# A layer norm's last multiply moved from GpSimd to VectorE inside a pipelined attention stage

## The reference, cut to what matters

```python
def _layernorm(x, axis=-1, eps=1e-05):
    m = jnp.mean(x, axis=axis, keepdims=True)
    v = jnp.var(x, axis=axis, keepdims=True)
    return (x - m) / jnp.sqrt(v + eps)
...
    q = (Q @ Wq.T + bq).reshape(b, vc, h, hd)
    k = (K @ Wk.T + bk).reshape(b, vc, h, hd)
    v = (V @ Wv.T + bv).reshape(b, vc, h, hd)
    atten = jnp.einsum('bqhd,bkhd->bhqk', q, k) / np.sqrt(hd)
    atten = jax.nn.softmax(atten, axis=3)
    out = jnp.einsum('bhqd,bdhv->bqhv', atten, v).reshape(b, vc, d_model)
    return out @ Wo.T + bo
...
x = _layernorm(x + _L0_xattn_ref(x, ctx_1024, ctx_1024, ...), axis=-1)
```

## Time and profile before

| | us |
|---|---|
| median of 3 runs | 2804.24 (2803.35 to 2806.08) |
| profiled execution, its own time | 2806.08 |
| its span in the profile | 2804.0 |
| mean granted TensorE clock | 0.990 |
| attention stage, roughly | 1618 to 2308 of the span |
| store of one step to the store of the next, in the loop | 84.5 |

### The profile page before, as it was taken

How to read it: one execution, slowest core, us unless ns; L and a number is a source line. 1 busy time by engine, 2 the same in 40 slices (tenths; PEclk the granted TensorE clock), 3 DMA queues, 4 the chain that set the end, 5 groups by cost and what they waited for, 6 DMA issues and landing times.

```text
span 2804.0 us, 42177 instructions
## 1 busy us (share of the span) xinstructions
PE 2692.1 (96%) x15200; PEld 2082.5 (74%) x15200; DVE 1529.3 (55%) x2566; ACT 1029.9 (37%) x2385; POOL 638.3 (23%) x564
## 2 busy tenths in 40 slices
PE   6999999999999999999999989999999979999998
PEld 4777777777778888888888767777777756777775
DVE  6887887787785221233133477777777762111222
ACT  6244244344344222122212255555555543222221
POOL 0643543553451100010001011333222331000000
PEclk9999999999999999999999999999999989999999
DMA  3011011101113101110112120111011213211111
GB/s 134 16 46 45 8 37 45 36 9 45 45 46 137 61 0 60 60 60 14 46 60 94 37 100 9 53 60 60 22 45 60 79 46 125 86 45 45 45 45 45
DMA packets 85417, 147.81 MB, mean 53 GB/s; under 512 B 3968, under 2 KB 17920, under 8 KB 85344
## 3 DMA queue, kind: packets, MB, share of 16 engines
q1 hardware_dynamic: 85344, 146.84, 15.1%
HBM read 113.27 MB, written 33.55 MB: 52 GB/s over the span
## 4 chain that ended last, share of the span: by engine, by line
PE 84%; DVE 9%; issue 2%; ACT 2%; DMA 1%; POOL 1%; DVEq 0%; SPq 0%; POOLq 0%; ACTq 0%
PE ps L75 22%; PE ps L77 21%; PE ps L76 21%; PE ps L1640 4%; PE ps L1919 4%; PE ps L730 3%; PE ps L1652 2%; DVE mx_cv L537 2%; DVE at_pT L1504 1%; PE ps L1631 1%; DVE mx_m L545 1%; PE ps L706 1%; PE ps L718 1%; DVE at_r_hl L1511 1%; PE ps L1660 1%
## 5 line engine op out<-in xcount | busy, mean ns | idle before, releaser
L1354 ACT ACTIVATE at_pr<-ps,at_nm 128x256 f32<-128x256 f32 x512 | 236.4, 475 | 199.7 <-DVE at_nm L1498 199.7
L1056 DVE TENSOR_TENSOR gm_m_lo<-gm_m,gm_m_hi 128x512 fp32r<-128x512 f32 (+1 forms) x88 | 61.0, 693 | 416.9 <-ACT gm_m_hi L973 416.9
L75 PE MATMUL ps<-sh_u_hi,gm_gu_hi 128*128 128x512 f32 (+1 forms) x704 | 275.4, 391 | 1.6 <-DVE gm_gu_lo L213 1.6
L77 PE MATMUL ps<-sh_u_hi,gm_gu_lo 128*128 128x512 f32 (+1 forms) x704 | 275.3, 391 | 0.0
L76 PE MATMUL ps<-sh_u_lo,gm_gu_hi 128*128 128x512 f32 (+1 forms) x704 | 275.1, 391 | 0.0
L1504 DVE COPY at_pT<-ps 128x512 f32<-128x512 f32 x256 | 176.0, 687 | 129.3 <-PE ps L1640 125.0
L967 ACT ACTIVATE gm_sg<-ps 128x512 f32<-128x512 f32 (+1 forms) x88 | 52.6, 598 | 520.9 <-PE ps L77 520.9
L75 PE MATMUL ps<-sh_u_hi,qm_w_hi 128*128 128x512 f32 x512 | 201.4, 393 | 3.9 <-DVE qm_w_lo L211 3.9
L76 PE MATMUL ps<-sh_u_lo,qm_w_hi 128*128 128x512 f32 x512 | 199.9, 390 | 0.0
L77 PE MATMUL ps<-sh_u_hi,qm_w_lo 128*128 128x512 f32 x512 | 199.7, 390 | 0.0
L1640 PE MATMUL ps<-sh_ident,at_pr 128*128 128x128 f32 x1024 | 164.5, 284 | 35.0 <-DVE at_pT L1504 31.9
(11 more groups left out here) (237 smaller groups left out, 6322.9 us busy)
## 6 DMA issues: line engine op xcount, KB each, us to landing
sh_xf<-x_scratch SPq DMA_DIRECT2D x16, 1024.0 KB, 7.5
sh_xf<-in_x SPq DMA_DIRECT2D x8, 1024.0 KB, 7.3
mx_xr<-in_x SPq DMA_DIRECT2D x8, 1024.0 KB, 6.3
h_scratch<-mx_xr SPq DMA_DIRECT2D x8, 1024.0 KB, 5.2
sh_xf<-h_scratch SPq DMA_DIRECT2D x8, 1024.0 KB, 7.9
gm_xr<-in_x SPq DMA_DIRECT2D x8, 1024.0 KB, 7.3
gm_r<-h_scratch SPq DMA_DIRECT2D x8, 1024.0 KB, 5.9
x_scratch<-gm_r SPq DMA_DIRECT2D x8, 1024.0 KB, 5.1
```

The source lines that it names most:

```text
L75: nc.tensor.matmul(out, l_hi, r_hi, start=first, stop=False)
L77: return nc.tensor.matmul(out, l_lo, r_hi, start=False, stop=last)
L1354: A(pr[h][:, t, :], SC[h][:, SEQ * t:SEQ * t + SEQ], ACT.Exp, bias=nm[:, 4 * n + h, t:t + 1], accum_out=sums[:, 2 * b + t, 4 * g + h:4 * g ...
```

## The change

The four instructions that subtract the mean and multiply by 1/std go from GpSimd to VectorE. On VectorE they stand in round 5, between `take_pT(i, 5, 1)` and `invert`. The fourth `statistics` and `gather` go from round 5 to round 4, and GpSimd computes 1/std behind its first `out_low`, ahead of the context's third and fourth tile. Behind the last step the same four instructions run on VectorE as well.

```diff
     def gpsimd(pool):
-        def normed(i):
-            residual_rstd(nc, pool, s, i, mv, var, rstd, eps, mhalf)
-            pool.wait_ge(s["mv"], TT)
-            pool.wait_ge(s["rstd"], i + 1)
-            for t in range(TT):
-                nc.gpsimd.tensor_scalar(r[:, t, :], r[:, t, :], mv[:, t, 0:1], rstd[:, t:t + 1], ALU.subtract,
-                                        ALU.mult).then_inc(s["ln"], 1)
...
             out_low(i, 0)
+            if not step_0(i):
+                residual_rstd(nc, pool, s, i - 1, mv, var, rstd, eps, mhalf)
             if not final(i):
                 context_low(pool, i + 1, 2)
                 context_low(pool, i + 1, 3)
             out_low(i, 1)
-            if not step_0(i):
-                normed(i - 1)
             out_low(i, 2)
...
         out_low(NP - 1, HG - 1)
-        normed(NP - 1)
+        residual_rstd(nc, pool, s, NP - 1, mv, var, rstd, eps, mhalf)
...
     def vector(dve):
+        def normed(i):
+            dve.wait_ge(s["rstd"], i + 1)
+            for t in range(TT):
+                V.tensor_scalar(r[:, t, :], r[:, t, :], mv[:, t, 0:1], rstd[:, t:t + 1], ALU.subtract,
+                                ALU.mult).then_inc(s["ln"], 1)
...
                     elif n == 4:
-                        for t in range(1, 3):
+                        for t in range(1, 4):
                             statistics(i - 1, t, before(i, 5 + t) + 1)
+                        gather(i - 1)
                     elif n == 5:
-                        statistics(i - 1, 3, before(i, 8) + 1)
-                        gather(i - 1)
+                        normed(i - 1)
...
         gather(n)
+        normed(n)
```

## The result

The changed kernel takes 2829.32 us (median of 4 runs, 2826.48 to 2830.53), the kernel before 2804.75 in the same comparison. The ratio is 1.0087, with a 95% interval of 1.0075 to 1.0100: slower by 24.6 us (21 to 28). The forecast was 2825 with a range of 2813 to 2837. So the sign and the size hold. The way there does not hold in three places (the clock, the last step, and what stands behind it), and their errors, of either sign, largely cancel.

A forecast was written before the change was run, and what follows sets the result against it. PE was taken to set the pace, waiting only for DVE's copy of a turned tile. Six loop steps at 3.21 us (19.3) plus the last step's 1.6 gave +20.9 us, so 2825 us, range 2813 to 2837.

The forecast's parts named there:

- the clock: Behind PE's round 5 wait of 3.0 us: at most two falls to half clock were allowed, each losing 1.6 us.
- the last step: Final attention step: +0.89 in round 4, +0.34 in round 5 after 0.6 us of cover, plus round 7; +1.6 us.
- what stands behind it: After the final step: stores and weight loads come some 7 us earlier, nobody on PE's path waits for them; no effect.
- Which copies bound PE: Loop rounds 4 and 5: PE already waits for DVE's copy, so DVE work added ahead of it adds to PE's time.
- Round 4: One bn_stats and four bn_aggr added right before the copy PE waits for; +0.89 us per step.
- The turns with POOL: Round 5: DVE and POOL alternate one instruction each, holding the first two tensor_scalar; the later cast runs free.
- Round 5: Four tensor_scalar ahead of the copy, two held by POOL, start the copy 1.97 us later; PE's wait becomes about 3.0 us.
- DVE keeping its turn through all four: Round 5 alternative: the four tensor_scalar run without POOL's out_low in between; copy +1.69 us later.
- Rival 2: POOL does not hold tensor_scalar: round 5 costs only +0.11 us, total 2811 to 2814 us; chance 0.09.
- Round 7: Earlier residual lets bias adds follow out_low at once and hold DVE's subtract, delaying the copy; +0.35 us per step.
- the likeliest case: Whole kernel: the summed forecast with at most two falls of the clock, 2820 to 2830 us; chance 0.58.
- rival 1: The clock falls behind PE's round 5 wait; 2835 us if in every loop step; chance 0.25 of three or more falls.

The follow-up runs named there:

- the statistics alone: Kernel before, with only the fourth bn_stats and the four bn_aggr moved from round 5 to round 4, GpSimd still normalising; 2808.07 us, ratio 1.0016.
- the kernel with POOL out of the way: Changed kernel, with GpSimd starting its round 5 work only after DVE's invert of that round, in steps with a layer norm; 2815.31 us, ratio 1.0040.
- the filler experiment: Changed kernel, with eight unused 128x512 matmuls at the head of round 6 in steps 1 to 6, in PE's wait; 2822.58 us, ratio 1.0067.
- the last layer norm alone: Kernel before, with only the four tensor_scalar behind the last step moved to DVE; 2798.36 us, ratio 0.9981.

## Why the prediction was right, and where it was not

**Which copies bound PE, and that DVE's queue ahead of them goes to PE one to one.** Right. Round 4 was put at +0.89 us and took 0.98, in the changed kernel and in the statistics alone.

**The turns with POOL.** Right in kind: the first and second tensor_scalar are held, `out_low` in between, the cast is free. Round 5 was put at +1.97 and took 1.69. The step that was off is "a DVE instruction held by POOL ends at POOL's end plus its own free length less 0.12 to 0.14 us": for the tensor_scalar it is 0.28 us behind POOL's end, 0.54 less 0.26. Twice 0.12 makes up most of the difference of 0.28. That 1.69 is also the number that the prediction had for DVE keeping its turn through all four is chance: `out_low` ends ahead of the second tensor_scalar, which takes 1.50 us. The rule of the Trainium skill, page "SBUF — State Buffer", section "Who interferes with whom", which names tensor_scalar among the instructions that can take the shared port pair, is borne out: 1.18 and 1.50 us for 0.54, and 0.54 again once POOL was held back. Rival 2, no holding, fell with it; the kernel with POOL out of the way shows what it would have cost, 0.10 us in round 5 for my 0.11.

**Round 7.** Right: the residual came early, the bias adds followed `out_low` at once and held the subtract (1.16 us), and with the adds held back the wait went. +0.35 was forecast, 0.21 came.

**The clock.** Here the likeliest case was wrong and rival 1 came true. I had let at most two falls pass, since my wait of 3.0 us lay between one of 3.11 with a fall and one of 2.79 without. The wait became 2.73 us, below both, and the clock fell in every step. And the wait of 2.79 us itself, the one for the last `out_low`, is 2.78 us in the changed kernel and in the kernel with the tensor_scalar in round 6, with 0.68 and 0.50 over the five us behind it, for 1.00 before and with the bias adds held back. So the length of one wait doesn't decide. In the loop PE waits a further 1.17 us some 12 us before; whether that matters isn't shown. The price of a fall was put at 1.6 us and is 1.2 in the loop (88.76 less 87.60), which the filler experiment shows to be the clock's. So the case that came true had 0.25 and the number 2835; the median came out nearer to the 2825 of the case that didn't.

**The last step.** Put at +1.6, it took +5.6. The step left out the low parts of the next stage's weights, which are DVE instructions with two SBUF inputs too, behind the copy in round 7. I had counted the earlier bias adds for the subtract only. With the bias adds held back, 3.1 of the 5.6 us were gone, but 1.5 of these are the half clock behind the last wait for `out_low`, which the adds may have nothing to do with. The step is also 5.3 us longer with POOL out of the way and 5.4 with the tensor_scalar in round 6, so the turns with POOL in rounds 4 and 5 can't be the whole of it. The cause of the rest stays open; it wasn't taken apart.

**Behind the last step.** The sentence "nobody on PE's path waited for those" was wrong. PE waited 3.88 us in the MLP, and I had read the row that told it, DVE's idle 4.87 us, as cover. It was the mark of the late weights themselves. The change gains 5.6 us there, as the last layer norm alone shows.

Put together: 6 x (0.98 + 1.69 + 0.21) = 17.3, the clock and what remains of the step 6 x 1.32 = 7.9, the last step 5.6, the MLP -5.6, ahead of it -0.8: 24.4, the difference of the two spans. My 20.9 was the first of these too large (19.3), the second and fourth missing, the third too small (1.6). Term by term the errors are -2.0, +7.9, +4.0, -5.6 and -0.8 us: some 20 us of them leave 3.5. That rounds 4, 5 and 7 cost what they cost was foreseen; that the total came so close is in good part luck.

## What to carry to other kernels

Where two engines wait in turn for one copy, what counts is where in the queue an instruction stands, not how busy its engine is: the same four instructions cost 3 us and more a step ahead of the copy for which PE waits and nothing in the idle time ahead of another. When work moves to DVE, look at what POOL runs at that moment, and at what POOL will run earlier since the work is gone. An idle time on a helper engine isn't cover until one has asked what ended it.

## What the runs showed of the hardware

Where DVE's tensor_scalar, cast or two-input subtract meets POOL's work, the two take turns, one instruction each, also with both queues full: 1.18, 1.47, 1.50 us for 0.54, 1.28, 0.54 in round 5. Not all of DVE's work is held: a bn_stats beside POOL's context instruction takes 0.68 us (two with POOL idle take 1.28), and the copy out of PSUM at 1939.63 in the changed kernel, beside another, 0.69. A 128x16 subtract with two SBUF inputs is held like a large one, 1.16 to 1.20 us for 0.17. A tensor_scalar that was held ends 0.28 us behind POOL, a subtract of the same size 0.56 us. PE came back at half clock for about 3 us behind waits of 2.7 us in a stretch with one other wait, of 1.17 us; another wait of 2.78 or 2.79 us, at one place of the program, had half clock behind it in two kernels and full clock in two others. What decides is open. Matmuls put into the wait, with no use, kept the clock at 1.00 and made the kernel some 7 us faster.

The fastest version here, with POOL behind the invert and all side work of DVE in its idle time, takes 2775.5 us: 1.0% less than the kernel before and 1.9% less than the changed one. With PE busy for 406.7 of 407.4 us in its loop, what remains in this stage's loop is PE's own work.
